# Cross-attention on one core: where the softmax division is done

## The reference, cut to what matters

```
qh = (q @ Wq.T + bq)   # 16 heads of 16
kh = (k @ Wk.T + bk);  vh = (v @ Wv.T + bv)   # k = v = context, 77 rows
attn = softmax(einsum('bhqd,bhkd->bhqk', qh, kh) * scale, axis=-1)
out = einsum('bhqk,bhkd->bhqd', attn, vh)     # heads side by side again
x = x + (out @ Wo.T + bo)
```

## Time and profile before

| | |
|---|---|
| median of 3 runs | 3282.31 us (3278.56 to 3284.23) |
| the profiled execution, span from first to last instruction | 3282.5 us |
| PE busy | 2918.6 us, 89% |
| DVE busy | 2077.4 us, 63% |
| ACT busy | 1409.4 us, 43% |
| POOL busy | 1502.3 us, 46% |
| the cross-attention (its PE work) | from 2201 to 2494 us |

### The profile page before, as it was taken

The page is one execution under the profiler, slowest core; times in us unless marked ns, Lnnn a source line. Parts: engine busy times, 40 slices in busy tenths (PEclk is TensorE's granted clock), DMA queues, the critical chain, the costliest instruction groups (busy, mean ns, idle before and its releaser), DMA issues. The chain is left out here.

```text
span 3282.5 us, 43728 instructions
## 1 busy us (share of the span) xinstructions
PE 2918.6 (89%) x15459; PEld 1876.9 (57%) x15459; DVE 2077.4 (63%) x3809; ACT 1409.4 (43%) x2698; POOL 1502.3 (46%) x1189
## 2 busy tenths in 40 slices
PE   6898898898887679799999999988886999999998
PEld 2343343343334565455555555546665888888887
DVE  7899899898998646566666666647883222222222
ACT  5667767757753302254545454545551111111111
POOL 5787787787784541233333333236763111111111
PEclk8999999999989689899999999989997999999999
DMA  7135135135130171122222222220114665565662
GB/s 228 59 97 155 59 99 155 60 96 155 64 102 0 67 244 41 28 47 49 53 65 59 49 49 49 47 72 14 47 53 171 190 207 178 190 206 177 186 211 61
DMA packets 280263, 339.71 MB, mean 103 GB/s; under 512 B 84547, under 2 KB 237311, under 8 KB 280047
## 3 DMA queue, kind: packets, MB, share of 16 engines
q1 hardware_dynamic: 256799, 303.41, 31.0%
q0 software_dynamic: 16704, 27.21, 3.5%
q10 hardware_dynamic: 6544, 6.30, 0.6%
HBM read 231.55 MB, written 104.80 MB: 102 GB/s over the span
## 5 line engine op out<-in xcount | busy, mean ns | idle before, releaser
L542 POOL TENSOR_TENSOR mb_drive<-mb_dtx,mb_b_rep 128x1024 f32<-128x1024 f32 x255 | 597.2, 2356 | 191.0 <-DVE mb_pD L439 94.8
L853 PE MATMUL mb_pY<-mb_hc,ident 128*128 128x512 f32 x1024 | 509.4, 624 | 53.3 <-DVE mb_hc L456 53.1
L1969 DVE TENSOR_REDUCE at_nm_of<-at_pS 128x1 f32<-128x128 f32 x756 | 402.5, 555 | 201.5 <-PE at_pS L1961 108.8
L3126 POOL DMA_INDIRECT out<-et_y,et_to x71 | 111.9, 1577 | 659.9 <-DVE et_y L3180 402.5
L3170 DVE TENSOR_TENSOR et_mT<-et_silu,et_pU 128x512 f32<-128x512 f32 (+1 forms) x160 | 100.4, 628 | 470.8 <-ACT et_silu L3141 470.8
L853 PEld LDWEIGHTS mb_pY<-mb_hc,ident 128*128 128x128 f32 x1024 | 193.8, 198 | 330.4 <-issue 188.4
L3141 ACT ACTIVATE et_silu<-et_pG 128x512 f32<-128x512 f32 (+1 forms) x160 | 87.8, 549 | 651.0 <-PE et_pU L3202 651.0
L1957 PE MATMUL at_pS<-at_kT,at_qT 64*128 64x128 f32 x756 | 301.4, 446 | 71.1 <-DVE at_nm_of L1969 61.1
L598 ACT ACTIVATE mb_pD<-mb_dt,mb_a_neg 128x512 f32<-128x512 f32 x384 | 259.6, 688 | 154.5 <-DVE mb_hc L456 143.2
L439 DVE TENSOR_TENSOR_SCAN mb_pD<-mb_pD,mb_drive 128x1024 f32<-128x1024 f32 x128 | 292.8, 2288 | 46.6 <-ACT mb_pD L596 44.5
L445 DVE TENSOR_TENSOR_SCAN mb_pD<-mb_pD,mb_carried,mb_drive 128x512 f32<-128x512 f32 x256 | 314.4, 1273 | 7.6 <-ACT mb_pD L598 7.6
(11 more groups left out here) (491 smaller groups left out, 5292.6 us busy)
## 6 DMA issues: line engine op xcount, KB each, us to landing
t_wg<-in_t_wgT SPq DMA_DIRECT2D x40, 1024.0 KB, 6.2
t_wu<-in_t_wuT SPq DMA_DIRECT2D x40, 1024.0 KB, 8.9
t_wd<-in_t_wdT SPq DMA_DIRECT2D x40, 1024.0 KB, 11.3
mb_b_rep<-mb_rows SPq DMA_DIRECT2D x64, 512.0 KB, 5.7
mb_c_rep<-mb_rows SPq DMA_DIRECT2D x64, 512.0 KB, 5.0
t_h_sorted<-blank SPq DMA_DIRECT2D x6, 4160.0 KB, 21.5
t_h_sorted<-blank SPq DMA_DIRECT2D x18, 1170.0 KB, 6.5
t_h_sorted<-blank SPq DMA_DIRECT2D x12, 1040.0 KB, 6.2
```

The lines of the kernel that those rows point to most:

```text
L542: nc.gpsimd.tensor_tensor(drive[G % RINGS][:, :, :], dtx[:, m, :].unsqueeze(1).to_broadcast([P, 2, CH]), b_rep[:, 2 * j:2 * j + 2, :], ALU ...
L853: last = nc.tensor.matmul(pY[:, :], K.ident[:, :], hc[G % RINGS][:, k, :], start=False, stop=(j == PAIRS - 1 and k == 1))
L1969: nc.vector.tensor_reduce(nm_of[:, w0 // 512, a, qb:qb + 1], score_bank(t, k)[:, 0:w1 - w0], axis=AX.X, op=ALU.max, negate=True).then_inc( ...
```

## The change

The exponentials are transposed as they are. Beside each value product, PE makes one more product of the same transposed exponentials with a stationary operand of ones, `one_v`, shaped as the values are: it gives, in columns 256 to 511 of `pM`, the sum of a head's exponentials, repeated for each of the head's 16 features. DVE then takes 128 x 256 reciprocals of those columns and multiplies columns 0 to 255 with them into `mixedT`. The sums and the 16 reciprocals on DVE, the multiplication on POOL and the copy on ACT go. `divide(n - 3)` stands at DVE's step n, right behind `subtract(n)`.

```diff
-        total, inv = sb("total", [P, NH]), sb("inv", [P, NH])
+        one_v, inv = sb("one_v", [CTX, 2, 2 * HD]), sb("inv", [P, D])
@@ DVE
-            def sums(n):
-                if n > 0:
-                    eng.wait_ge(s_inv, n)
-                eng.wait_ge(s_exp, 2 * n + 2)
-                nc.vector.tensor_reduce(total[:, :], e[n % 3][:, :, :], axis=AX.X, op=ALU.add).then_inc(s_tot, 1)
-
-            def invert(n):
-                eng.wait_ge(s_tot, n + 1)
-                if n > 0:
-                    eng.wait_ge(s_nrm, 2 * n)
-                nc.vector.reciprocal(inv[:, :], total[:, :]).then_inc(s_inv, 1)
+            def divide(n):
+                eng.wait_ge(s_pv, 2 * n + 2)
+                nc.vector.reciprocal(inv[:, :], pM[:, D:2 * D]).then_inc(s_inv, 1)
+                eng.wait_ge(s_inv, n + 1)
+                if n >= 2:
+                    eng.wait_ge(s_O, n - 1)
+                nc.vector.tensor_tensor(mixedT[n % 2][:, :, :].rearrange("p k q -> p (k q)"), pM[:, 0:D], inv[:, :], ALU.mult).then_inc(s_mx, 1)
@@ DVE, set up once
+            for a in range(2):
+                nc.vector.memset(one_v[:, a, a * HD:(a + 1) * HD], 1.0)
+                nc.vector.memset(one_v[:, a, (1 - a) * HD:(2 - a) * HD], 0.0)
@@ DVE, step n
+                if 3 <= n < NT + 3:
+                    divide(n - 3)
...
-                if 1 <= n <= NT:
-                    sums(n - 1)
...
-                if 1 <= n <= NT:
-                    invert(n - 1)
@@ POOL
-            def spread(n):
-                eng.wait_ge(s_inv, n + 1)
-                for m in range(KD):
-                    em = e[n % 3][:, m * HM:(m + 1) * HM, :]
-                    nc.gpsimd.tensor_tensor(em, em, heads(inv, m).unsqueeze(2).to_broadcast([P, HM, CTX]), ALU.mult).then_inc(s_nrm, 1)
...
-                if 1 <= n <= NT:
-                    spread(n - 1)
@@ ACT
-            def mixed(n):
-                eng.wait_ge(s_pv, 2 * n + 2)
-                if n >= 2:
-                    eng.wait_ge(s_O, n - 1)
-                nc.scalar.copy(mixedT[n % 2][:, :, :], pM[:, 0:D].rearrange("p (k q) -> p k q", k=KD)).then_inc(s_mx, 1)
...
-                if 2 <= n < NT + 2:
-                    mixed(n - 2)
@@ PE
-                eng.wait_ge(s_nrm, 2 * n + 1 + g // 2)
+                eng.wait_ge(s_exp, 2 * n + 1 + g // 2)
@@ PE, weigh(n, m)
                 for a in range(2):
                     for j in range(4):
-                        last = nc.tensor.matmul(pM[32 * j:32 * j + 32, m * P:(m + 1) * P], v[:, b, m * 4 + j, a, :],
+                        nc.tensor.matmul(pM[32 * j:32 * j + 32, m * P:(m + 1) * P], v[:, b, m * 4 + j, a, :],
+                                         eT[j][:, 2 * m + a, :], start=(a == 0), stop=(a == 1), skip_group_check=True)
+                for a in range(2):
+                    for j in range(4):
+                        last = nc.tensor.matmul(pM[32 * j:32 * j + 32, D + m * P:D + (m + 1) * P], one_v[:, a, :],
                                                 eT[j][:, 2 * m + a, :], start=(a == 0), stop=(a == 1), skip_group_check=True)
                 last.then_inc(s_pv, 1)
```

More of the change, by code:

```diff
@@ L2518, in _cross_attention @@
         s_in, s_set, s_kT, s_kTc, s_kp, s_vp, s_vc = (sem(n) for n in ("in", "set", "kTp", "kTc", "kp", "vp", "vc"))
-        s_A, s_read, s_S, s_top, s_sub, s_exp, s_tot, s_inv, s_nrm, s_pv, s_mx, s_O, s_res = (
-            sem(n) for n in ("A", "read", "S", "top", "sub", "exp", "tot", "invs", "nrm", "pv", "mx", "O", "res"))
+        s_A, s_read, s_S, s_top, s_sub, s_exp, s_inv, s_pv, s_mx, s_O, s_res = (
+            sem(n) for n in ("A", "read", "S", "top", "sub", "exp", "invs", "pv", "mx", "O", "res"))
         s_st, s_mv, s_ve, s_rs, s_rows, s_ve0, s_rs0, s_xn = (sem(n) for n in ("st", "mv", "ve", "rs", "rowsn", "ve0", "rs0", "xns"))
@@ L2527, in _cross_attention @@
         bank = lambda name, ch: pT[NTH[name, ch] % 2]
-        heads = lambda T, m: T[:, m * HM:(m + 1) * HM]
         block = c.enter_context(nc.Block(no_gpsimd_drain=True))
```

## The result

Over 20 runs each on one chip, the kernel after took 3288.32 us (median; 3275.24 to 3297.18), the kernel before 3279.05 (3266.32 to 3287.24): a ratio of 1.0025, interval 1.0014 to 1.0036. The profiled run of after took 3293.38 us, its span 3291.8. The change makes the kernel slower, by 0.14 to 0.36% in the first comparison; the second alone wouldn't tell it from no change.

A forecast was written before the change was run, and what follows sets the result against it. PE was taken to carry the stage's steady load, with DVE's delays on top in three chunks. The terms 7.4 + 5.4 + 0 gave +12.8 us on the span of 3282.5: 3295 us, range 3285 to 3309.

The forecast's parts named there:

- no change to be measured: Rival, chance 0.10: ones cost 0.6 to 0.8 us a tile, or larger waits go; 3283 to 3289 us.
- the signs: Right if reciprocals 1.7 to 1.9 us, ones about 35 busy, 3 us waits gone, chunks 34 to 34.5, clock near 1.0.
- The ones: On PE, 16 more products a tile cost 1.01 us a tile, 32.3 us over the stage.
- Up to the first chunk: Up to the scores at 2281.28: eight tiles, 8.1 us more, less 0.7 at the start: +7.4 us.
- The five chunks: From 2281.28 to 2445.77: four chunks of 34.2 us and a last of 33.1, +5.4 us.
- The end: Behind 2445.77: four more tiles weighed, 4.0 us, hidden by PE's waits: 0.
- What goes: DVE loses 1.67 us a tile; POOL's two multiplications, 76.5 us, and ACT's copy go, their time uncounted.
- The 3.02 us wait: PE's wait ahead of the product with Wo for DVE's late addition; the long chunks give it back.
- The cast's: DVE's stall in the cast, forecast to go with POOL's multiplications.
- DVE's terms: Reciprocal over 256 columns 1.8 us, multiplication 0.410; DVE gains 2.2 and loses 1.7 a tile: plus 0.55 us.
- DVE becomes the bound: Rival, chance 0.16: DVE ties with PE; a reciprocal of 2.2 us gives chunks of 35.9, 3304 us, up to 3311.
- faster: Rival, chance 0.07: products with ones nearly free, under 0.6 us a tile; chunks about 31.0 us, 3275 us in all.

The follow-up runs named there:

- the second comparison: The kernel after, timed once more beside the one before without an edit: 3292.08 us, ratio to before 1.0013 (0.9993 to 1.0033).
- early_add: The kernel before, with DVE's addition to the residual moved ahead of the router's choice and shares: 3295.61 us, ratio to before 0.9994.
- recip_twice: The kernel after, with the same reciprocal taken twice, the first result unused: 3348.78 us, ratio to before 1.0161.
- scatter_spread: The kernel after with its reciprocal taken twice, and POOL issuing two indirect DMAs in each of four turns: 3312.12 us, ratio to before 1.0087.
- narrow_bias: The kernel before, with POOL adding the bias to 2 of 256 columns only: 3285.18 us, ratio to before 0.9976.
- early_sums: The kernel before, with DVE's sums, addition to the residual and small reciprocals moved ahead of the router's choice: 3290.33 us, ratio to before 0.9993.
- turned_inverse: The kernel after, its divisors made by DVE's sums and small reciprocals, ACT copies and PE transpositions instead of ones: 3285.09 us, ratio to before 0.9996.
- ones_left_out: The kernel after without the products with ones, the reciprocal reading columns 0 to 255: 3265.23 us, ratio to before 0.995.

## Why the forecast was right, and where its steps missed

Slower by over 0.2% had 0.81, and the ratio is 1.0025, though its interval and that of the second comparison reach under 1.002. The forecast of 3295 was 6.7 us above the median of 3288.32, inside the range. The mechanism, PE carrying the ones on a stage that it sets, is shown: taking the ones alone away takes 17.9 us off the stage. Its sizes were off, nearly all to one side.

That the number fell inside is in part luck. The forecast's own account, the stage, was +8 to +18, and the stage grew by 4.8 (up to 6.9, by its first 36 us). The profiled executions lie 9.3 us apart, as the medians do, and 4.1 of that lies ahead of the stage, where nothing was changed. And 3288.32 also lies in the range of the rival "no change to be measured" (3283 to 3289): its ones at 0.6 to 0.8 us a tile were a little too cheap, but its other half, that more waits go than I counted, is what the runs show. The truth lies between that rival and the forecast. Of the signs, the reciprocals of 1.7 to 1.9 us, the end of the 3 us waits, the equal chunks and the clock of 1.00 came; the chunks of 32.7 us lie between the 34 to 34.5 that were to show the forecast right and the 31 to 32 that were to show it wrong, and the group of ones was 41.2 us busy, not 35.

- *The ones.* 0.87 us a tile, not 1.01: 27.8 us, not 32.3. I reasoned that 16 more products of the same shape cost as much as the first 16. The first 16 include the lead-in and the run-out to the product with Wo; the groups in between follow at 0.44 us. This is 4.5 us of the 8.0 by which the sum was too high.
- *Up to the first chunk*, +5.05 against +7.4. To the scores of the fifth tile, one `weigh` with ones on the way, after is 1.06 us ahead (35.19 against 36.25), so the start gave 0.87 + 1.06 = 1.9 us, not 0.7. That this is the change's doing isn't shown: early_add, which still divides on POOL, has the same gain there (34.15). The seven tiles behind them then cost 6.1, 0.87 each: there, PE runs through, as the step said.
- *The five chunks*, -1.75 against +5.4: the term that failed. Its base was the quickest chunk of before less 1.14 us of waits, 30.2. Without the ones the chunk is 30.53, so this base was even a little low. What was wrong is that the ones were added whole to it: 1.3 of the 3.48 us of a measured chunk are absorbed, 1.1 of them in waits that PE has without the ones, for DVE's addition and subtraction and for one copy. An engine that is 91% busy still had room. Ones that cost 0.14 us a tile less take another 0.6 off a chunk, and the base, too low, adds 0.3: together the 1.5 us between 34.2 and 32.7.
- *The end*, +1.5 against 0. I took all four tiles' ones, 3.5 us, to be hidden by PE's waits. In after the waits for the last copies of exponentials are 2.5 us instead of 3.8 and the 1.0 for DVE's addition is gone: 2.3 hidden, the rest shows.
- *What goes.* The 3.02 us wait, the slow product behind it and the lower clock went, as forecast, and so did DVE's 2.30 us stall. The cast's did not, against the prediction. In three chunks it now meets POOL's addition of the bias:

```profile
2392.72 1.67 DVE L2617 CAST xa_index_f<-xa_index 128x8 f32<-128x8 uint32 x1
```

```profile
2392.02 2.34 POOL L2770 TENSOR_TENSOR resid<-resid,xa_bo 128x1024 f32<-128x1024 f32 x1
```

The cast ends at 2394.39, POOL's addition at 2394.36. It costs PE nothing here: PE waits for DVE nowhere in the chunks.
- *DVE's terms.* The reciprocal is 1.75 us (1.81 from the slope of the earlier trace rows; 0.41 was the lower bound), the multiplication 0.425 (0.41). A slope over narrow rows of the same operation held up to eight times their width. The eight divide steps a column of the Trainium skill, "VectorE: DVE Perf Modes", section "First, the fixed hardware budget", would have given 2.13, an estimate from that page; the trace disagrees, with 1.75, 6.8 ns a column. By the rule of the Trainium skill, "SBUF — State Buffer", section "Who interferes with whom", neither new operation should be held up by POOL, and of 64 in the stage none was: the longest took 1.76 and 0.43 us. In after that is a weak test. Ten of them met POOL at work, all on its normalisation (`xa_xn`), and beside that before's casts took only 0.20 and 0.25 us too; the long ones, 1.81 us, met POOL's multiplication. The test is in recip_twice and scatter_spread: six reciprocals and seven multiplications began while POOL added the bias, the operation beside which after's casts took 1.65 to 1.67 us, and none took over 1.75 and 0.43.
- *The rival "DVE becomes the bound"* did not come. DVE is 28.7 us busy in a chunk, not 31.3, since the sum counted 3.8 us of stalls of which some 1.5 are left, and it waits for the logits. scatter_spread shows what it would have been: 3.5 us of reciprocal a tile, chunks of 35.4 to 38.5.
- *The rival "faster"* had its turning point at 0.6 us a tile. By the runs everything else gives 13.1 us, so ones that cost the stage under 13.1 of the 17.9 us they do, some 0.6 us a tile by that proportion, would have made it faster; with 2.1 us less to give, for the clock at the start, some 0.5. The point was about right, though both of its terms were too large: 19.5 us to be absorbed, and 1.01 us a tile.

## What to carry to other kernels

When an operation is added to the engine that sets the pace, read its price from the starts of neighbouring groups, not from busy sums, and then ask what part of it falls into that engine's remaining short waits: leaving the operation out and adding it to the old kernel bracket this from both sides (17.9 and 11.4 us here, for 27.8 of work). A detour over a third engine, as POOL's multiplication was, can cost more by its chain and by holding up the small operations of a neighbour (12.5 to 14.6 us) than the work on DVE that takes its place (1.4); what undid the gain here is the new work on PE. And compare by the stage: of after it repeated to 0.1 us, while where it starts moved by up to 21. But look at it piece by piece: the first 36 us of before differ by 2.1 us from those of kernels with the same work.

## What the runs showed of the chip that was not expected

- Stretches in which PE, ACT and DVE stand or get on in steps of 1.43 us together, while POOL issues a burst of eight indirect DMAs: 5 to 6 us of each chunk in recip_twice, and once in narrow_bias, early_add and early_sums, whose last part is 5 to 9 us longer. Spreading the same DMAs over more turns removed them (scatter_spread). After issues the same eight in a row in each chunk, and before in its last part, without any such stretch, so the burst alone isn't enough. What the second condition is stays open; no run here separates it. One candidate is that the engines' instructions come late, since many of the waits are marked "issue", which is time in which the profile shows nothing waited for; nothing here tests it.
- The granted clock fell on PE in turned_inverse in the middle of work without a gap right ahead of it (0.68 over 5.40 us, behind a stretch at 1.00), each chunk again, and not in ones_left_out, whose PE does the same but for the transpositions and waits as long in a chunk (2.8 us). I have no cause to show for it.
- Which of POOL's operations holds up small ones on DVE matters more than how long it is. Beside POOL's multiplication or addition over two inputs (2.3 to 2.4 us) the casts of the router took 1.65 to 1.81 us; beside its normalisation (4.8 us) they took at most 0.47, in all these kernels. Moving DVE's addition ahead of the held operations gained nothing in two versions: PE then waited for something else that stood behind them.
